# Layer 1 softmax attention on 128 partitions: sixteen heads side by side

## What is computed

```python
HID, NH, NKV, HD = 128, 16, 4, 8          # 16 query heads, 4 key heads, 8 numbers each
h = _rmsnorm(x, ln1_w)
qkv = jnp.einsum('bsh,oh->bso', h, wqkv)
q, k = _apply_rope(q, cos, sin), _apply_rope(k, cos, sin)
k, v = jnp.repeat(k, 4, axis=2), jnp.repeat(v, 4, axis=2)
scores = jnp.einsum('bqhd,bkhd->bhqk', q, k) * HD ** (-0.5)
scores = jnp.where(causal, scores, finfo.min)
attn = jnp.einsum('bhqk,bkhd->bqhd', softmax(scores), v).reshape(B, S, 128)
x = x + jnp.einsum('bso,ho->bsh', attn, wo)
```

## Time and profile before

| | |
|---|---|
| median of three runs | 1994.01 us (1991.31 to 1997.19) |
| profiled execution, span | 2015.3 us |
| TensorE busy | 1735.7 us, 86% |
| VectorE busy | 1298.6 us, 64% |
| ScalarE busy | 1000.1 us, 50% |
| DMA | 168.32 MB, mean 84 GB/s |

### The profile page before, as it was taken

One profiled execution on the slowest core, in us unless ns is written; L12 is line 12 of the kernel. 1 busy time (PEld: TensorE's weight loads), 2 busy tenths in 40 slices (PEclk: granted clock), 3 DMA queues, 4 the chain that ended last, 5 costly groups with the idle time before them and its releaser, 6 DMA issues.

```text
span 2015.3 us, 61260 instructions
## 1 busy us (share of the span) xinstructions
PE 1735.7 (86%) x23044; PEld 1256.4 (62%) x23060; DVE 1298.6 (64%) x3615; ACT 1000.1 (50%) x2258; POOL 254.2 (13%) x267
## 2 busy tenths in 40 slices
PE   5999999998898888985898898987888898888856
PEld 3665666665665665653767666674666666666656
DVE  5677767775666656654677666774756766666525
ACT  3444444444554555553555654555445555554335
POOL 0000000000000000012101111011111121220054
PEclk9899999998999999997999999999999999999979
DMA  4333333332221222223122221220031121221244
GB/s 169 129 139 138 138 138 138 138 138 79 66 66 40 66 65 65 64 79 105 50 65 68 74 76 55 66 62 29 26 93 49 44 65 51 66 66 48 76 125 124
DMA packets 97374, 168.32 MB, mean 84 GB/s; under 512 B 15145, under 2 KB 65465, under 8 KB 93882
## 3 DMA queue, kind: packets, MB, share of 16 engines
q1 hardware_dynamic: 87322, 142.18, 20.9%
q0 software_dynamic: 9888, 23.71, 4.0%
HBM read 87.01 MB, written 78.80 MB: 82 GB/s over the span
## 4 chain that ended last, share of the span: by engine, by line
PE 53%; DVE 15%; issue 12%; ACT 11%; SPq 4%; DMA 2%; another core or an unknown queue 1%; DVEq 1%; POOL 0%; POOLq 0%; ACTq 0%
PE psum L1001 5%; PE psum L844 4%; PE psum L878 3%; PE psum L991 3%; PE psum L1306 3%; PE psum L1196 3%; PE psum L1294 2%; PE psum L889 2%; PE psum L1040 2%; PE psum L925 2%; PE psum L1093 2%; PE psum L1221 2%; PE psum L929 2%; PE psum L1086 2%; PE psum L1125 2%
## 5 line engine op out<-in xcount | busy, mean ns | idle before, releaser
L1546 ACT ACTIVATE pts<-psum 128x512 f32<-128x512 f32 x192 | 99.1, 603 | 170.6 <-PE psum L1040 170.0
L718 POOL DMA_INDIRECT rows<-h,recA x64 | 64.2, 1004 | 843.8 <-DVE recA L1788 717.4
L2050 DVE TENSOR_REDUCE mneg<-psum 128x2 f32<-128x512 f32 (+1 forms) x192 | 119.1, 682 | 53.3 <-PE psum L1020 35.0
L1001 PE MATMUL psum<-wall,xT_s 128*128 128x512 f32 x256 | 125.9, 638 | 0.0
L878 PE MATMUL psum<-txT,wall 128*128 128x128 f32 x864 | 118.6, 281 | 6.1 <-DVE st L2057 3.0
L742 POOL DMA_INDIRECT rows<-xn,recC x32 | 36.5, 1139 | 677.2 <-DVE recC L2239 620.3
L889 PE MATMUL psum<-wall,tg 128*128 128x128 f32 (+1 forms) x720 | 107.6, 284 | 16.0 <-ACT tg L1429 10.5
L878 PEld LDWEIGHTS psum<-txT,wall 128*128 128x128 f32 x864 | 110.8, 198 | 9.0 <-issue 4.2
L1155 PE MATMUL psum<-xT_s,wall 128*128 128x256 f32 x512 | 115.7, 379 | 0.0
L889 PEld LDWEIGHTS psum<-wall,tg 128*128 128x128 f32 x720 | 93.1, 196 | 25.8 <-DVE tg L1736 13.6
L1155 PEld LDWEIGHTS psum<-xT_s,wall 128*128 128x128 f32 x512 | 96.1, 190 | 13.2 <-issue 0.8
(11 more groups left out here) (275 smaller groups left out, 4285.1 us busy)
## 6 DMA issues: line engine op xcount, KB each, us to landing
wall<-in_wB SPq DMA_DIRECT2D x84, 384.0 KB
outs<-pbd SPq DMA_DIRECT2D x16, 1024.0 KB, 8.0
mixed_rows<-pbd SPq DMA_DIRECT2D x16, 899.5 KB, 10.5
wall<-in_wD SPq DMA_DIRECT2D x24, 578.0 KB
tx<-rows SPq DMA_DIRECT2D x132, 64.0 KB
rows<-pbd SPq DMA_DIRECT2D x64, 128.0 KB, 1.7
rows<-pbd SPq DMA_DIRECT2D x8, 1024.0 KB, 3.9
outs<-ty SPq DMA_DIRECT2D x108, 64.0 KB, 1.6
```

The source lines that it names most:

```text
L1001: mm(bank(f"{name}{t}{c}"), xnT[:, t * P:(t + 1) * P], wqkv0[:, off + c * 512:off + (c + 1) * 512], start=True, stop=True).then_inc(*fills ...
L1546: af(pT[:, n, :], bank(f"e{n}"), ACT.Exp, scale=float(HD) ** -0.5).then_inc(*frees(f"e{n}"))
L2050: ins = v.tensor_reduce(mneg[:, int(n >= 4), col:col + hs], sc, AX.X, ALU.max, negate=True)
```

## The change

The sixteen heads stand side by side on the 128 partitions, 8 rows each: key head g has rows 32g to 32g + 31, its four query heads inside. One product each gives queries and turned queries, keys and turned keys (keys repeated four times), so that `wrope` has four slices. VectorE makes two copies of the queries (`qx`): in each 32 rows, copy 0 keeps rows 16 to 31 (heads 2 and 3) and copy 1 rows 0 to 15 (heads 0 and 1), the rest being zero and later taking the maxima. ScalarE makes four copies of the keys (`kx`), each with all but one head's 8 rows zero, and a one in the row that takes the head's maximum. A score product then has 32 rows and 256 columns, and the transposed one 32 rows and 128 columns, one for each head. `v9` and `ones32` are laid out the same way, four times with zeros, so that values and sums of all heads gather in one bank `pa` of 256 columns. The sums, their inverse and `aT` are 128 columns wide instead of 512, and the output product is one matmul for each 128 tokens. ScalarE's making of `kx` stands between its work on q and the norm of x2; it is waited for ahead of the first scores.

```diff
-        names += [f"rq{j}" for j in range(2)] + [f"rs{j}" for j in range(2)] + ["rk", "v9"]
+        names += ["rk", "rq", "v9"]
...
-        wrope = wa[:, 3072:4352].rearrange("p (a n) -> p a n", a=10)
+        wrope = wa[:, 3072:3584].rearrange("p (a n) -> p a n", a=4)
...
@@ TensorE @@
-                    for r in range(GR):
-                        last = mm(bank("wo")[:, t * P:(t + 1) * P], aT[:, r, t * P:(t + 1) * P], woR[:, r, :], start=(r == 0), stop=(r == GR - 1))
+                    last = mm(bank("wo")[:, t * P:(t + 1) * P], aT[:, t * P:(t + 1) * P], woR, start=True, stop=True)
...
+                            rows = slice(32 * g, 32 * g + 32)
+                            queries = slice(0, P) if part == 0 else slice(P, N)
+                            scores_of = bank(use).rearrange("p (b c k) -> p b c k", b=2, c=2)
+                            dst = scores_of[:, pair, :, :] if part == 0 else scores_of[:, :, i, :]
+                            last = mm(dst, qx[rows, pair, queries], kx[rows, 2 * pair:2 * pair + 2, key:key + P], start=False, stop=(i == 1))
...
-                    for g, use in enumerate(uses):
-                        rows = slice(32 * g, 32 * g + HD + GR)
-                        mm(bank(use), kr[rows, kt * P:(kt + 1) * P], qr[rows, :, t * P:(t + 1) * P],
-                           start=(kt != t), stop=True).then_inc(*fills(use))
+                    for j in range(GR):
+                        for g, use in enumerate(uses):
+                            rows = slice(32 * g, 32 * g + 32)
+                            last = mm(bank(use)[:, j * P:(j + 1) * P], kx[rows, j, kt * P:(kt + 1) * P], qx[rows, j // 2, t * P:(t + 1) * P],
+                                      start=(kt != t and j == 0), stop=(j == GR - 1))
...
-                                last = mm(bank(f"{name}{t}")[32 * g:32 * g + 32, :], v9[:, part // 2, g, :] if name == "pn" else ones32[:, :], pT[:, n, :],
-                                          start=(part == parts[0]), stop=(part == parts[-1]))
+                                    values = v9[:, NKV * (part // 2) + g, j, :] if i == 0 else ones32[:, j, :]
+                                    last = mm(bank(f"pa{t}")[32 * g:32 * g + 32, i * P:(i + 1) * P], values, pT[:, n, j * P:(j + 1) * P],
+                                              start=(part == parts[0] and i == 0 and j == 0), stop=(part == parts[-1] and i == 1 and j == GR - 1))
...
                 pe.wait_ge(*given("rope_ready"))
+                pe.wait_ge(*given("kx_ready"))
                 scores(0)
@@ ScalarE @@
+                act.wait_ge(*given("kr_ready"))
+                for j in range(GR):
+                    ins = af(kx[:, j, :], kr[:, :], ACT.Identity, scale=cols[:, KEEP + j:KEEP + j + 1], bias=cols[:, ONE + j:ONE + j + 1])
+                ins.then_inc(*signals("kx_ready"))
                 gate_norm()
...
-                    af(rden[:, t, :, :], bank(f"pd{t}").rearrange("p (r n) -> p r n", r=GR), ACT.Ln).then_inc(*frees(f"pd{t}"))
+                    af(rden[:, t, :], bank(f"pa{t}")[:, P:2 * P], ACT.Ln).then_inc(*signals("act_chain"))
@@ VectorE @@
+                v.tensor_tensor(rp[:, 2:4, :], bank("rk").rearrange("p (a n) -> p a n", a=2), ropec, ALU.mult).then_inc(*frees("rk"))
...
+                v.tensor_tensor(kr[:, :], rp[:, 2, :], rp[:, 3, :], ALU.add).then_inc(*signals("kr_ready"))
...
+                v.tensor_tensor(rp[:, 0:2, :], bank("rq").rearrange("p (a n) -> p a n", a=2), ropec, ALU.mult).then_inc(*frees("rq"))
...
+                v.tensor_tensor(qr, rp[:, 0, :], rp[:, 1, :], ALU.add).then_inc(*signals("dve_chain"))
...
+                    ins = v.tensor_scalar(qx[:, pair, :], qr, cols[:, 44 - pair:45 - pair], None, ALU.mult)
...
-                    v.tensor_tensor(aT[:, :, t * P:(t + 1) * P], bank(f"pn{t}").rearrange("p (r n) -> p r n", r=GR), rden[:, t, :, :], ALU.mult).then_inc(*frees(f"pn{t}"))
+                    v.tensor_tensor(aT[:, t * P:(t + 1) * P], bank(f"pa{t}")[:, 0:P], rden[:, t, :], ALU.mult).then_inc(*frees(f"pa{t}"))
...
-                    for r in range(GR):
+                    for pair in range(2):
...
-                        ins = v.scalar_tensor_tensor(out=qr[:, r, ts], in0=bank(f"mT{t}")[:, 0:P], scalar=cols[:, 44 + r:45 + r], in1=qr[:, r, ts], op0=ALU.mult, op1=ALU.add)
+                        ins = v.scalar_tensor_tensor(out=qx[:, pair, ts], in0=bank(f"mT{t}")[:, 0:P], scalar=cols[:, 43 + pair:44 + pair], in1=qx[:, pair, ts], op0=ALU.mult, op1=ALU.add)
```

More of the change, by code:

```diff
@@ L2104, in attention0 @@
                 dve.wait_ge(*read_out("rk"))
[L2105 to L2107 removed]
+                v.tensor_tensor(kr[:, :], rp[:, 2, :], rp[:, 3, :], ALU.add).then_inc(*signals("kr_ready"))
+                dve.wait_ge(*filled("rq"))
@@ new lines, in attention0 @@
+                dve.wait_ge(*filled("v9"))
+                values = bank("v9")[:, 0:NT * NKV * HD].rearrange("p (a o d) -> p a o d", o=1, d=HD)
+                for first in (2 * HD, 2 * 32):
+                    places = v9s[:, first:first + NT * NKV * P].rearrange("p (a x) -> p a x", a=NT * NKV)
+                    pair = places[:, :, 0:2 * (32 + HD)].rearrange("p a (b e) -> p a b e", b=2)[:, :, :, 0:HD]
+                    ins = v.tensor_copy(pair, values.to_broadcast([P, NT * NKV, 2, HD]))
@@ L2387 @@
     ang = np.concatenate([ang, ang], -1).T
-    woR = np.zeros((P, GR, D), np.float32)
-    for g in range(NKV):
-        for a in range(GR):
-            woR[32 * g:32 * g + HD, a] = I["L0_ffn_wo"].T[(GR * g + a) * HD:(GR * g + a + 1) * HD]
+    woR = I["L0_ffn_wo"].T
     ropec = np.zeros((P, 2, N), np.float32)
-    for g in range(NKV):
-        ropec[32 * g:32 * g + HD, 0] = np.cos(ang)
-        ropec[32 * g:32 * g + HD, 1] = np.sin(ang) * np.r_[-np.ones(HD // 2), np.ones(HD // 2)].astype(np.float32)[:, None]
+    ropec[:, 0] = np.tile(np.cos(ang), (P // HD, 1))
+    ropec[:, 1] = np.tile(np.sin(ang) * np.r_[-np.ones(HD // 2), np.ones(HD // 2)].astype(np.float32)[:, None], (P // HD, 1))
     wD = np.concatenate([I["L1_ffn_W1"], I["L1_ffn_b1"].reshape(E, 4, P).transpose(0, 2, 1),
```

147 lines of the change are left out of this document (68 added, 79 removed).

## The result

The changed kernel takes 1934.9 us (median of 4 runs, 1929.9 to 1937.4) against 1992.7 for the kernel before on the same chip: the ratio is 0.9703, with a 95% interval of 0.9686 to 0.9720. That is 57.8 us less. The forecast was 54.4 less, 1940. Its profiled execution took 1937.4 us, 2.5 above the median, with a span of 1935.4, while the one of before had a span of 2015.3, 21 above its median.

A forecast was written before the change was run, and what follows sets the result against it. TensorE was taken to bound the kernel, with 53% of the chain of waits. Savings of 41.6 (plain), 4.4 (expert), 7.4 (last) and 1.0 (first) sum to 54.4 us, off the 1994.0 median: 1940, range 1920 to 1965.

The forecast's parts named there:

- Rotary and output products: TensorE in front of attention: fewer records save 2.6 and 1.4 us in plain iterations, nothing in expert ones.
- Scores, transposed scores, weighted sums: TensorE in attention: scores gain 0.1 us; short packed records at 29 ns leave sums unchanged, transposed scores unchanged at 34 ns.
- slower rival: Short packed matmuls don't pack, 52 ns a record in sums and transposed scores: about +8 us, 2002; chance 0.07.
- VectorE, ScalarE, tight front: Before h2: VectorE's 6.2 us become about 3.6, slack falls to 0.1 to 0.3; 0.3 us an iteration lost.
- first rival: VectorE and ScalarE take the front; v and h2 waits eat all but VectorE's 2.6 us: 1952 us, chance 0.22.
- The tail: ScalarE's ln and exp of the sums and VectorE's L2042 shrink, shortening TensorE's wait before q: 0.9 us gained.
- Plain iterations: Eight layer 1 iterations without expert tiles: 5.2 us saved in each, 41.6 in all, ending near 43.7 us.
- Expert iterations: Six with expert tiles: front saving lost to h2 wait of about 8 us; 8.4 minus 4 for clock, 4.4 together.
- that sign of being wrong: Expert iterations under 60 us would count against the forecast, which expected them near 62.
- The low clock: After the longer h2 wait in expert iterations: 1.3 us more at lower level, half lost, 0.7 each, 4 in all.
- The last iteration and the stage behind it: Last iteration with experts, no next x to wait for, and following stage: 4.0 + 1.0 + 1.0 + 1.4, 7.4 us saved.
- The bounds of the terms: Whole kernel: the terms put the time between 1926 (no tight front, longer idle costless) and 1948 us.

## Why the prediction was right, and where it was not

**Rotary and output products.** Forecast 2.6 and 1.4 us; the rows show 1.72 for the eight records left and 0.53 for the four: 2.6 and 1.3. Put back, they cost 3.8 us of a plain iteration. Right there; in expert iterations 3.5 us were saved up to h2.

**Scores, transposed scores, weighted sums.** I took 29 ns a record and no change; it was 28 for the sums, 34 for the transposed scores. Right, and for the reason given, L1190's overlap of tiles; that it hangs on the tiles taking turns was not in the forecast. The slower rival (records that don't pack, 2002) was a real cliff beside the path taken: one turned loop gives 1998. The Trainium skill's 60 cycles a matmul ("TensorEngine Tiling (Array Packing)", Instruction Overhead), by an estimate 25 ns at 2.4 GHz, don't add up from record to record: 64 columns came every 14 ns.

**VectorE, ScalarE, tight front.** Forecast 3.6 us from the first product to the end of the sum that makes x2, 6.2 before. Measured, 286.29 to 289.88, 3.6. The wait before h2 in plain iterations is still nought, and h2 is ready 0.3 us before TensorE takes it. The four copies into kx took 2.08 us, not four times about 0.3, and this cost nothing. The run with kx in pieces finds ScalarE's cover at 0.4 us. I took 0.3 us of loss; the plain iteration of 43.5 instead of 43.7 leaves about 0.1, by difference. Right, slightly too careful. The first rival (1952) falls with it.

**The tail.** Forecast 0.9, from the wait before q: 1.45 became 0.37, so 1.1, of which 0.1 to 0.2 came back as a longer wait before xn. Right in size. I had not seen which block's logarithm it was.

**Plain iterations.** Forecast 5.2 each, measured 5.4.

**Expert iterations.** Forecast 4.4 us in all, 2.1 measured against an ordinary execution. The mechanism is the one forecast: from the record's store to h2 it is about 20 us before and after (means 20.1 and 20.1), so that what the front saves goes into the wait, 1.5 are gained behind it (forecast 1.4), 0.9 lost to the clock (forecast 0.7). The runs with x early and with the wait filled show both. The wait grew by 2.6 (2.3 to 4.9), not by 4.0: the front saved 3.5, and q comes 0.9 later behind the record (2.1 to 2.9 us), since at full clock the record comes 1.5 sooner after h2 and q only 0.7. What was most wrong is the *level*: I read 3.92 us of wait and 17.5 us from record to x as the program's own, and they were one execution's, whose span stood 21 us above the median. So I forecast a wait of 8 us and a period near 62, and counted a period under 60 as proof against me. They were 5 us and 60.1, and two of the five stood under 60 (59.3 and 59.2): that sign of being wrong came true, of the level and not of the mechanism. A difference of two profiles would have told that this change brought 2.9 us in each of these iterations, where it brought 0.5. The forecast survived since it counted the change by its steps, from the execution's own time, and took the same sum off the median.

**The low clock.** Forecast 1.3 us more at the lower level, half lost. The five stretches lost 2.3 us each to the clock after and 1.4 before, so 0.9 more, where 0.7 was forecast. The term was slightly too small. It wasn't seen to what it leads: that more work is faster there. The Trainium skill ("TensorE: Matmul & The Clock Gate", Why this matters for your kernels) asks that bursts not be parted by idle gaps; the run with the wait filled agrees, with 10.4 us.

**The last iteration and the stage behind it.** Forecast 7.4, measured 2.6 in this pair and 4.8 by the means above. This is the term that failed. Up to the output product 4.9 us were saved, where the forecast has 6.0: TensorE's own work gave 3.9 instead of 5.0, and its wait for ln, exp and product the 1.0 forecast (1.64 became 0.60). And the stage behind has a wait for h2 as well, which the forecast left out; it took back 0.9 of the product's 1.4. In this pair the clock took 2.8 more (the stretch from h2 to the next wait's end, before again and after):

```profile
893.17:918.12 24.95, 8.42 (x59) 7.87 (x59) 13.06 (x60) 5.20 (x13) 10.30 (x12) 0.73 0.40 125
```

```profile
838.39:866.10 27.71, 11.18 (x59) 10.46 (x59) 13.06 (x60) 5.20 (x13) 10.71 (x12) 0.58 0.35 113
```

The same 59 instructions take TensorE 2.76 us longer. In the pair with x early, where that stretch took 27.6 us before and 27.5 after, the same place took 92.7 us against 98.4, 5.7 saved. How much clock this stage gets differs between executions, and what decides it wasn't found.

**What made up for it.** 3.0 us more in plain iterations than forecast (one of them slow in that profile of before), and 5.9 us at the start and in layer 2, where nothing was changed. The total is nearer to the forecast than its parts are, and that is luck: terms that were too high by 7.1 us in the expert iterations and the last one met 8.9 that came from elsewhere, two thirds of it from code that the change leaves alone.

**The bounds of the terms.** The lower one, 1926, doesn't follow from the two terms named: 0.3 us in eight iterations and 4 for the clock take 6.4 off 1940, which gives 1934. The range that was stated is wider, 1920 to 1965, and doesn't use it.

## What to carry to other kernels

Before a wait is priced from one profile, hold the profiled span against the median of the runs: here 21 us of difference sat mostly in two places, layer 2 and the wait on which the forecast turned. The same holds for a difference of two profiles: the last iteration's gain was 2.6 in one pair and 5.7 in another. Work saved in front of a late transfer is lost twice, once to the wait and once to the clock after it; move the transfer's issue first (SyncE's edits were worth 47 us here, nearly as much as the change), and only then shorten what stands before it. When a long matmul is cut into short packed ones, let neighbours in the instruction stream go to different tiles, and watch the number of instructions in the loop: both keep all the work the same and each can cost as much as the change gave.

## What the runs showed of the hardware that I had not expected

- Packed float32 records of 128 columns in four column tiles came every 28 ns when the tiles took turns, every 64 ns when eight in a row went to one tile; with 64 columns, every 14 ns.
- A loop with 1746 recorded TensorE instructions an iteration stalled in each iteration (37.9 us of idle time put down to issue before one group of records in the whole kernel, 252 instruction transfers in the kernel against 138), one with 1801 as well, and loops with 1362, 1618 and 1673 ran without a transfer once they were steady. The Trainium skill ("Runtime: NRT & Kernel Launch", Instruction fetch mechanics) has instructions streamed in blocks of 16 KiB, and the transfers agree with the size: 2.26 MB in 138 is 16.4 KB. It says that a taken branch out of the two nearest blocks forces a fetch. The trace disagrees: the loop of eight iterations with 1362 instructions each had no transfer from its second iteration on, and no wait of TensorE of more than 0.05 us put down to issue.
- Twenty-four useless records before the wait in each of six iterations made a kernel 10.4 us faster, with the clock at 1.00 instead of 0.93 in the stretch behind it.
- ScalarE's copy with a scale and a bias by partition cost 0.49 us for 256 columns and 0.33 for 64 in a row of such instructions, while pieces of 32 columns of a logarithm, which names neither by partition, came every 0.1 us. Which of the differences counts wasn't tried.
